# Deformable-convolution stage: the convolution moved ahead of the gathers, all row turns between the second and third spread, and the arguments of the offsets in two buffers

## The chip, the cores and the metric

The kernel is written by hand for one core of a Trainium2 chip, in fp32 throughout. The metric is device time in microseconds of one execution. The kernel before was timed three times: median 1808.21 us, 1806.97 to 1809.94.

A core has a matrix engine (TensorE, PE in the profile), whose weight loads are listed apart (PEld), and three engines for elementwise work: VectorE (DVE), ScalarE (ACT) and GpSimd (POOL). SyncE (SP) only issues DMAs here. Every engine has its own stream of instructions, and streams meet at semaphores alone. Small scalar instructions (register arithmetic, branches, semaphore waits that stand by themselves) are carried out by the engine's sequencer, which hands matmuls and weight loads on to the engine.

## What is computed

`x` is 8 x 32 x 128 x 128. Two residual layers follow each other, each on a normalized input:

```python
x = x + _L0_conv_ref(_gn(x), ...)   # spectral terms along H and W, and a 1x1 mix of channels
x = x + _L1_conv_ref(_gn(x), ...)   # deformable 3x3 convolution

# _L1_conv_ref, cut:
om = conv3x3(x, w_om) + b_om                    # 27 maps: 18 offsets, 9 masks
off, mask = om[:, :18], sigmoid(om[:, 18:])
ys, xs = off + tap + pixel                      # a sampling point for every tap and pixel
vals = bilinear(x, ys, xs) * mask               # all 32 channels
out = einsum('bckhw,ock->bohw', vals, weight) + bias
```

The change touches only the second layer.

## The kernel before

The eight images go in two groups of four, so that 4 images x 32 channels fill the 128 partitions. After the first layer (about the first 180 us) a pipeline of 130 steps runs, 65 for each group (64 pairs of image rows and one more to finish). A step works on several pairs at once, in different stages. In step N:

- `offsets(N+3)` (L1122): the 3x3 convolution for the 27 maps, into the PSUM bank `pM`. ACT adds the bias (L655), `turn_offsets` (L1132) turns the result so that pixels stand on partitions, ACT takes the sigmoid of the masks (L666), and DVE subtracts the grid from the offsets, into `U` (L889). That is called the *subtraction* below.
- For pair N+2, ACT makes the bilinear hats from `U`: absolute value in place (L645) and 1 minus it, cut at zero, into `HT` (L648). POOL multiplies them by the masks (L546) and makes the products of the y hats and x hats (`product`, L511).
- For pair N+1, DVE turns the products (`turn`, L838).
- For pair N, three `spread` stages (L1076) lay the turned coefficients out as matrices in the PSUM tile `pE`, and ACT and DVE copy each of them, half each, into `A` (`table`, L633 and L832). POOL cuts the input window into strips (`cut_tiles`, L523), PE turns them in four *turns* (`turn_rows`, L1110, into `pR` or `pVV`), and ACT copies these into `XT` (`turned`, L638). Then three `gather` groups (L1097, of 6, 5 and 5 tiles) multiply `XT` by `A`; ACT and DVE copy the result out (`samples`, L628 and L827).
- For pair N-1, `convolve` (L1156) applies the 3x3 weights into `pVV`, and DVE adds bias, input and the part begun before (`output`, L849 and L854). DVE's increment of `conv_read` frees `pVV`.

Nothing plans this at run time: each engine's order is written out by hand in its `step` function. On PE it was: spread 0, convolve (N-1), spread 1, offsets (N+3), spread 2, turns 2 and 3 of N, turn_offsets, gather groups 0 to 2, turns 0 and 1 of N+1. On PE the steps 2 to 126 are one hardware loop with one step as its body, and the first and last steps are written out (`steps`, L282 to L307); DVE and SP have two steps in a loop body, ACT and POOL four. At the end of a body the sequencer runs an addition, a compare-and-branch and a further register instruction at L304.

Which PSUM banks a stage uses is given by these two lines; a group in `pV` (the two banks of `pVV`) has to wait for `output`, and one in `pE` for the tables of the third spread:

```python
pG = [pV, [pE[:, 0:512], pE[:, 512:1024]], [pE[:, 1024:1536], pE[:, 1536:2048]]]
pT = [pR, pV[0], pV[0], pR]
```

## Time and profile before

| | |
|---|---|
| median of 3 runs | 1808.21 us |
| the profiled execution | 1805.23 us, of which the span is 1803.3 us |
| PE busy | 94% of the span |
| DVE / ACT / POOL busy | 74% / 65% / 49% |
| step of the loop, spread 0 to the next spread 0 | 1006.82 to 1018.59 us: 11.77 us |
| granted TensorE clock | full from about 275 us to 1763 us |

PE's busy share counts every moment at which some matmul is in flight, so it hides the time in which the array waits between two stages. What a stage costs is read here from the start of its first matmul to the start of the next stage's first matmul; these numbers add up to the step without gap or overlap. Instructions of the sequencer are not in the engine rows; the view of one source line lists them (as PEldq for PE).

### The profile page before, as it was taken

What the parts mean: (1) busy time and instruction counts of PE and PEld (TensorE: products, weight loads), DVE (VectorE), ACT (ScalarE), POOL (GpSimd) and SP (SyncE); (2) the same over time, 40 slices, a digit from 0 to 9 for tenths busy, and PEclk for the clock granted to TensorE, in tenths of its full rate; (3) what the DMA queues carried; (4) which work ended last, traced back from release to release, by engine and by line L of the source; (5) the groups of instructions that cost most, each with busy time, mean ns of one, the idle gap of its engine ahead of it and who ended that gap; (6) DMA issues with size and microseconds to landing.
All of it is one profiled execution on the core that took longest, in us unless ns stands there. A gap on an engine that the chain in (4) does not pass through costs nothing.

```text
span 1803.3 us, 159696 instructions
## 1 busy us (share of the span) xinstructions
PE 1703.3 (94%) x70913; PEld 1319.3 (73%) x70913; DVE 1329.7 (74%) x2056; ACT 1174.5 (65%) x1971; POOL 891.7 (49%) x1153
## 2 busy tenths in 40 slices
PE   8886479999999999999999999999999999999985
PEld 3521257888888888888888888888888888888874
DVE  7387457777777777777777777777777777777762
ACT  7148246667767667777667677667677677676652
POOL 0000245556555556555556555555555565555550
PEclk9799599999999999999999999999999999999997
DMA  9148632333333333333333233333333333333320
GB/s 385 26 186 364 228 120 74 98 97 87 88 93 97 97 96 87 88 95 97 97 95 89 81 94 97 97 93 87 89 96 97 97 89 88 93 96 97 97 57 13
DMA packets 161679, 195.95 MB, mean 109 GB/s; under 512 B 20288, under 2 KB 136672, under 8 KB 157536
## 3 DMA queue, kind: packets, MB, share of 16 engines
q1 hardware_dynamic: 161632, 195.34, 36.6%
q8 instruction: 28, 0.46, 0.1%
q14 instruction: 19, 0.16, 0.0%
HBM read 143.05 MB, written 52.22 MB: 108 GB/s over the span
## 4 chain that ended last, share of the span: by engine, by line
PE 90%; DMA 3%; DVE 2%; issue 2%; ACT 1%; POOL 0%; DVEq 0%; SPq 0%; POOLq 0%; ACTq 0%
PE pE L1076 18%; PE pVV L1156 16%; PE pE L1097 13%; PE pM L1122 10%; PE pVV L1097 8%; PE pR L1110 7%; PE pVV L1110 7%; PE pM L1132 4%; PE pE L991 3%; DMA xh_scratch<-stg 2%; PE pE L1048 1%; DMA win<-xh_scratch 1%; DVE big L799 1%; ACT stg L592 1%; PE pVV L1026 0%
## 5 line engine op out<-in xcount | busy, mean ns | idle before, releaser
L523 POOL COPY big<-win 128x480 f32<-128x480 f32 x520 | 290.6, 588 | 654.5 <-PE pVV L1110 438.3
L511 POOL TENSOR_TENSOR prod<-big 128x600 f32<-128x600 f32 (+1 forms) x489 | 498.5, 1040 | 29.6 <-POOL big L546 29.5
L633 ACT ACTIVATE big<-pE 128x768 f32<-128x768 f32 x390 | 334.8, 858 | 186.8 <-PE pE L1076 186.8
L832 DVE COPY big<-pE 128x768 f32<-128x768 f32 x390 | 372.9, 956 | 100.1 <-PE pE L1076 87.5
L838 DVE STREAM_TRANSPOSE big<-prod 128x768 f32<-128x768 f32 x390 | 377.4, 968 | 15.8 <-POOL prod L511 15.8
L1076 PE MATMUL pE<-big,sel_s 32*64 32x192 f32 x12480 | 358.8, 338 | 12.5 <-DVE big L832 10.3
L1076 PEld LDWEIGHTS pE<-big,sel_s 32*64 32x64 f32 x12480 | 220.2, 132 | 115.7 <-issue 64.0
L1156 PE MATMUL pVV<-big,wc 64*32 64x128 f32 x18720 | 295.7, 273 | 4.3 <-issue 3.3
L1156 PEld LDWEIGHTS pVV<-big,wc 64*32 64x32 f32 x18720 | 263.2, 106 | 46.5 <-issue 46.3
L1097 PE MATMUL pE<-big 60*32 60x72 f32 x20800 | 251.4, 232 | 17.1 <-issue 17.1
L1097 PEld LDWEIGHTS pE<-big 60*32 60x32 f32 x20800 | 230.2, 105 | 24.2 <-issue 18.9
L1122 PE MATMUL pM<-big,wom 96*32 96x256 f32 x3120 | 201.3, 391 | 19.7 <-DMA big<-xh_scratch 19.7
L827 DVE COPY big<-pE 128x360 f32<-128x360 f32 x260 | 138.5, 533 | 105.0 <-PE pE L1097 105.0
L628 ACT ACTIVATE big<-pE 128x360 f32<-128x360 f32 x260 | 122.4, 471 | 123.0 <-PE pE L1097 123.0
L638 ACT ACTIVATE big<-pR 128x512 f32<-128x512 f32 x260 | 156.3, 601 | 23.3 <-PE pR L1110 8.6
L1110 PE MATMUL pR<-ident,big 128*128 128x128 f32 x1040 | 165.0, 282 | 6.5 <-POOL big L523 4.6
L1122 PEld LDWEIGHTS pM<-big,wom 96*32 96x32 f32 x3120 | 89.0, 110 | 104.6 <-issue 58.4
L1110 PE MATMUL pVV<-ident,big 128*128 128x128 f32 x1040 | 165.1, 282 | 0.0
L827 DVE COPY big<-pVV 128x432 f32<-128x432 f32 x130 | 79.0, 608 | 112.9 <-PE pVV L1097 111.0
L1097 PE MATMUL pVV<-big 60*32 60x72 f32 x12480 | 156.5, 230 | 4.5 <-ACT big L638 2.0
L638 ACT ACTIVATE big<-pVV 128x512 f32<-128x512 f32 x260 | 153.2, 589 | 0.9 <-PE pVV L1110 0.8
L1097 PEld LDWEIGHTS pVV<-big 60*32 60x32 f32 x12480 | 137.5, 105 | 11.3 <-issue 5.4
(97 smaller groups left out, 1675.7 us busy)
## 6 DMA issues: line engine op xcount, KB each, us to landing
big<-xh_scratch SPq DMA_DIRECT2D x390, 136.0 KB
win<-xh_scratch SPq DMA_DIRECT2D x130, 408.0 KB, 3.7
xh_scratch<-stg SPq DMA_DIRECT2D x32, 544.0 KB, 3.4
big<-in_x SPq DMA_DIRECT2D x16, 1024.0 KB, 15.7
x_scratch<-big SPq DMA_DIRECT2D x16, 1024.0 KB, 4.4
x1r<-x_scratch SPq DMA_DIRECT2D x256, 64.0 KB, 3.0
out<-outs SPq DMA_DIRECT2D x256, 64.0 KB, 2.1
xh_scratch<-zero SPq DMA_DIRECT2D x4, 204.0 KB, 2.6
```

The lines of the kernel that those rows point to most:

```text
L511: made = nc.gpsimd.tensor_tensor(prod[:, kx, at:at + m, 0:SQ].rearrange("p m (a b) -> p m a b", a=NSH), hy.to_broadcast(shape), hx.to_broa ...
L523: last = nc.gpsimd.tensor_copy(strips[:, half * HTP:(half + 1) * HTP, h, 0:REG].rearrange("p t (r x) -> p t r x", r=WIN_R), tiles_of(q, h, ...
L633: nc.scalar.activation(*expanded(kx, 0), ACT.Copy).then_inc(e_read, 1)
L638: nc.scalar.activation(XT[:, k * 512:(k + 1) * 512], pT[k][:, 0:512], ACT.Copy).then_inc(xt_done, 1)
L827: nc.vector.tensor_copy(*evacuate(gi, 1)).then_inc(v_dve, 1)
L832: nc.vector.tensor_copy(*expanded(kx, 1)).then_inc(e_read, 1)
L838: nc.vector.transpose(PT[:, kx, :], prod[:, kx, :, :].rearrange("p m k -> p (m k)")) \
L1076: last = mm(o[:, i2::TILE_R], sel_s[part, i2 * KS + kx, :], src[:, i2::TILE_R, :, h * NTP:(h + 1) * NTP], start=True, stop=True)
L1097: last = mm(o[:, :, x:x + TILE_C, :], XT[part, t * P + b * C:t * P + (b + 1) * C], A[part, b * NTP + t, :], start=True, stop=True)
L1110: last = nc.tensor.transpose(pT[k][:, u * P:(u + 1) * P], strips[:, k * TPC + u, :, :].rearrange("p h x -> p (h x)"), ident[:, :])
L1122: last = mm(pM[b * C:(b + 1) * C, 0:PX], wom[:, kx, :], wino[0:KS * C, b, :, x0:x0 + W], start=(kx == 0), stop=(kx == KS - 1))
L1156: last = mm(pV[r][to:to + C, c:c + W], wc[part, PLACES[at][1] * KS + kx, o * C:(o + 1) * C], VS[part, m, kx, :], start=(at == same[0] and ...
```

## The change

Each of the five streams is put in another order, and four details follow from it:

- PE: spread 0, offsets (N+3), spread 1, turns 0, 1 and 2 of N, turn_offsets, turn 3, spread 2, convolve (N-1), gather groups 0, 1, 2. All four turns now belong to the pair of the step. Gather groups 0 and 1 go to `pE`, group 2 to `pV`; turn 2 goes to `pV[1]`.
- `U` has two buffers, and DVE makes the subtraction in the middle of its step, before the third table, not at its end. `output` goes from behind the first turn to behind the third.
- ACT makes the absolute value as before and the cut at zero (L648 before, L667 now) late in the step, behind the third table.
- POOL cuts the strips after the second and third product; SP loads the rows for the offsets one pair further ahead and later in its step.
- The first spread waits for the copies of all gather groups but the last; the last gather group waits for `conv_read`, and each gather group has its own wait on `xt_done`.

```diff
-        pG = [pV, [pE[:, 0:512], pE[:, 512:1024]], [pE[:, 1024:1536], pE[:, 1536:2048]]]
-        pT = [pR, pV[0], pV[0], pR]
+        pG = [[pE[:, 0:512], pE[:, 512:1024]], [pE[:, 1024:1536], pE[:, 1536:2048]], pV]
+        pT = [pR, pV[0], pV[1], pR]
...
# POOL, step
-                    cut_tiles(N + 1, 1 - s % 2, 0)
                     product(N + 1, (s + 1) % RING, 1)
                     product(N + 1, (s + 1) % RING, 2)
+                    cut_tiles(N + 1, 1 - s % 2, 0)
+                    cut_tiles(N + 1, 1 - s % 2, 1)
...
# DVE, step
-                if on[-1]:
-                    output(N - 1, 1 - s % 2, place)
                 if on[0]:
                     table(N, 1)
...
+                if on[3]:
+                    dve.wait_ge(msk_done, N + 4)
+                    wait(dve, lin_done, N + 2)
+                    wait(dve, reach_done, N + 2)
...
                 if on[1]:
                     turn(N + 1, 2)
+                if on[-1]:
+                    output(N - 1, 1 - s % 2, place)
...
# PE, spread
                 if kx == 0:
-                    wait(pe, v_act, n * NG)
-                    wait(pe, v_dve, n * NG)
+                    wait(pe, v_act, n * NG - 1)
+                    wait(pe, v_dve, n * NG - 1)
# PE, gather
                 if gi == 0:
+                    pe.wait_ge(e_read, (n * ROUNDS + ROUNDS) * 2)
+                if gi == NG - 1:
                     wait(pe, conv_read, n)
-                    pe.wait_ge(e_read, (n * ROUNDS + ROUNDS) * 2)
-                    pe.wait_ge(xt_done, n * TCH + 3)
-                    pe.nop(nofuse=True)
-                if gi == 1:
-                    pe.wait_ge(xt_done, n * TCH + TCH)
-                    pe.nop(nofuse=True)
+                pe.wait_ge(xt_done, n * TCH + 2 + gi)
+                pe.nop(nofuse=True)
...
# PE, step
                 if on[0]:
                     spread(N, 0)
+                if on[3]:
+                    offsets(N + 3)
+                if on[0]:
+                    spread(N, 1)
+                    for k in range(TCH - 1):
+                        turn_rows(N, k)
+                if on[3]:
+                    turn_offsets(N + 3)
+                if on[0]:
+                    turn_rows(N, TCH - 1)
+                    spread(N, 2)
                 if on[-1]:
                     convolve(N - 1)
                 if on[0]:
-                    spread(N, 1)
-                if on[3]:
-                    offsets(N + 3)
-                if on[0]:
-                    spread(N, 2)
-                    turn_rows(N, 2)
-                    turn_rows(N, 3)
-                if on[3]:
-                    turn_offsets(N + 3)
-                if on[0]:
                     for gi in range(NG):
                         gather(N, gi)
-                if on[1]:
-                    turn_rows(N + 1, 0)
-                    turn_rows(N + 1, 1)
```

The end of the loop body on PE, before: from the last matmul of `turn_offsets` through the gather groups (L1097) and the two turns (L1110) to the branch.

```order
L1132 MATMUL pM<-perm_s,om_s 128x9x4
L1085 REGISTER_ALU [waits conv_read]
L1086 REGISTER_ALU [waits e_read]
L1097 MATMUL pVV<-big 32x3x4x6 [waits xt_done]
L1097 MATMUL pVV<-big 32x3x4x6 x47
L1089 REGISTER_ALU
L1097 MATMUL pE<-big 32x3x4x6 [waits xt_done]
L1097 MATMUL pE<-big 32x3x4x6 x79
L289 ISA
L1104 ISA [waits xt_done]
L1110 MATMUL pR<-ident,big 128x128 [waits strips_done]
L1110 MATMUL pR<-ident,big 128x128 x3
```

The same place in the changed kernel, from the convolution (L1158) through the gather groups (L1096) to the branch.

```order
L1158 MATMUL pVV<-big,wc 32x128 x71
L1085 REGISTER_ALU
L1088 REGISTER_ALU [waits e_read]
L1096 MATMUL pE<-big 32x3x4x6 [waits xt_done]
L1096 MATMUL pE<-big 32x3x4x6 x47
L1088 REGISTER_ALU
L1096 MATMUL pE<-big 32x3x4x6 [waits xt_done]
L1096 MATMUL pE<-big 32x3x4x6 x39
L1088 REGISTER_ALU [waits conv_read]
L1096 MATMUL pVV<-big 32x3x4x6 [waits xt_done]
L1096 MATMUL pVV<-big 32x3x4x6 x39
L304 REGISTER_ALU
```

The gathers have one more place at which a register instruction and a wait cut their row of matmuls, and the loop's branch has moved from behind eight turns of 128 x 128 to right behind the last gather matmul.

The middle of the loop body on PE, before: spread 2 (L1076), turns 2 and 3 (L1110), `turn_offsets` (L1132).

```order
L1076 MATMUL pE<-big,sel_s 64x3x64 x15
L289 ISA
L1104 ISA [waits xt_done]
L1110 MATMUL pVV<-ident,big 128x128 [waits conv_read,strips_done]
L1110 MATMUL pVV<-ident,big 128x128 x3
L1110 MATMUL pR<-ident,big 128x128 [waits strips_done,xt_done]
L1110 MATMUL pR<-ident,big 128x128 x3
L1128 REGISTER_ALU
L1132 MATMUL pM<-perm_s,om_s 128x9x12 [waits om_act]
```

And now: behind spread 1 (L1077) come three turns (L1112), `turn_offsets` (L1134) and the fourth turn.

```order
L1112 MATMUL pR<-ident,big 128x128 x3
L1112 MATMUL pVV<-ident,big 128x128 [waits v_dve,v_act]
L1112 MATMUL pVV<-ident,big 128x128 x3
L1110 REGISTER_ALU
L1112 MATMUL pVV<-ident,big 128x128 [waits strips_done]
L1112 MATMUL pVV<-ident,big 128x128 x3
L1130 REGISTER_ALU
L1134 MATMUL pM<-perm_s,om_s 128x9x12 [waits om_act]
L1134 MATMUL pM<-perm_s,om_s 128x9x8
L1134 MATMUL pM<-perm_s,om_s 128x9x4
L1108 REGISTER_ALU
L1112 MATMUL pR<-ident,big 128x128 [waits xt_done]
```

The stages with 128 x 128 weights stood in two blocks and stand in one.

On DVE, the second half of a step before: third table (L832), third turn (L838), the copies of the gathers (L827), the subtraction (L889).

```order
L832 COPY big<-pE 128x2x64x6 [waits e_done]
L836 REGISTER_ALU
L838 STREAM_TRANSPOSE big<-prod 128x768 [waits e_done,prod_done]
L827 COPY big<-pVV 128x18x24 [waits v_done]
L827 COPY big<-pE 128x18x20 [waits v_done] x2
L883 REGISTER_ALU
L889 TENSOR_TENSOR big<-pM,cols_s 128x720 [waits reach_done,lin_done,msk_done]
```

And now: the subtraction (L880), third table (L831), third turn (L837), `output` (L848, L853), the copies (L826).

```order
L880 TENSOR_TENSOR big<-pM,cols_s 128x720 [waits reach_done,lin_done,msk_done]
L831 COPY big<-pE 128x2x64x6 [waits e_done]
L835 REGISTER_ALU
L837 STREAM_TRANSPOSE big<-prod 128x768 [waits e_done,prod_done]
L848 SCALAR_TENSOR_TENSOR outs<-pVV,bias_s,begun 128x256 [waits out_st1,conv_done]
L853 TENSOR_TENSOR begun<-pVV,x1r 128x256 [waits x1_ld1]
L826 COPY big<-pE 128x18x24 [waits v_done]
L826 COPY big<-pE 128x18x20 [waits v_done]
L826 COPY big<-pVV 128x18x20 [waits v_done]
```

Subtraction and `output` now both stand in the row of DVE work between the third spread and the gathers.

## Rows read from the trace of the kernel before

**Rows 1.** The page, groups: line, engine, count | busy us, mean ns of one | idle before.

```profile
L1097 PE MATMUL pE<-big 60*32 60x72 f32 x20800 | 251.4, 232 | 17.1 <-issue 17.1
```

**Rows 2.** Waits, 275 to 1740 us: engine, line, waited for, us in total, times, longest.

```profile
PEld pE L1076 <- DVE big L832: 51.1, 124, 0.4
```

**Rows 3.** Timeline of PE, one step: start us, length, line, output and input, count.

```profile
1006.82 0.91 PE L1076 MATMUL pE<-big,sel_s 32*64 32x192 f32 x32
1007.72 2.24 PE L1156 MATMUL pVV<-big,wc 64*32 64x128 f32 x144
1009.89 0.91 PE L1076 MATMUL pE<-big,sel_s 32*64 32x192 f32 x32
1010.73 1.50 PE L1122 MATMUL pM<-big,wom 96*32 96x256 f32 x24
1012.16 0.91 PE L1076 MATMUL pE<-big,sel_s 32*64 32x192 f32 x32
1013.00 0.66 PE L1110 MATMUL pVV<-ident,big 128*128 128x128 f32 x4
1013.49 0.60 PE L1110 MATMUL pR<-ident,big 128*128 128x128 f32 x4
1013.92 0.76 PE L1132 MATMUL pM<-perm_s,om_s 128*128 128x108 f32 x6
```

**Rows 4.** Timeline of PE, rest of that step and next spread; first row: last three of turn_offsets.

```profile
1014.21 0.47 PE L1132 MATMUL pM<-perm_s,om_s 128*128 128x72 f32 x3
1014.65 1.21 PE L1097 MATMUL pVV<-big 60*32 60x72 f32 x96
1015.75 1.88 PE L1097 MATMUL pE<-big 60*32 60x72 f32 x160
1017.56 0.66 PE L1110 MATMUL pR<-ident,big 128*128 128x128 f32 x4
1018.05 0.60 PE L1110 MATMUL pVV<-ident,big 128*128 128x128 f32 x4
1018.59 0.73 PE L1076 MATMUL pE<-big,sel_s 32*64 32x192 f32 x22
```

**Rows 5.** PEld: weight loads of gather groups 1 and 2, same step.

```profile
1015.72 1.73 PEld L1097 LDWEIGHTS pE<-big 60*32 60x32 f32 x160
```

**Rows 6.** PE's sequencer, 1014.4 to 1019.6 us: ns shortest/median/longest, first and last start.

```profile
L304 PEldq COMPARE_BRANCH  x1: 207/207/207, 1017.7 to 1017.7; - x1
L304 PEldq FUSED_REGOPS  x1: 59/59/59, 1018.0 to 1018.0; - x1
...
L289 PEldq FUSED_REGOPS  x2: 37/37/37, 1017.3 to 1018.9; - x2
L289 PEldq EVENT_SEMAPHORE  x2: 51/51/51, 1017.5 to 1018.2; - x2
```

**Rows 7.** PE's branch over all steps of the loop.

```profile
L304 PEldq COMPARE_BRANCH  x125: 76/208/223, 275.9 to 1736.5; - x125
```

**Rows 8.** Timeline of ACT and DVE in the step before.

```profile
1001.43 0.96 DVE L832 COPY big<-pE 128x768 f32<-128x768 f32 x1
...
1002.30 0.97 DVE L838 STREAM_TRANSPOSE big<-prod 128x768 f32<-128x768 f32 x1
...
1005.10 0.53 DVE L827 COPY big<-pE 128x360 f32<-128x360 f32 x1 [0.25 <-PE pE L1097]
...
1006.36 0.90 DVE L889 TENSOR_TENSOR big<-pM,cols_s 128x720 f32<-128x720 f32 x1
...
1006.99 0.59 ACT L638 ACTIVATE big<-pVV 128x512 f32<-128x512 f32 x1
```

**Rows 9.** Timeline at the first steps: masks, third subtraction, first table.

```profile
206.34 0.23 ACT L666 ACTIVATE msk<-pM 128x72 f32<-128x72 f32 x1 [1.59 <-PE pM L1132]
...
214.58 0.86 DVE L889 TENSOR_TENSOR big<-pM,cols_s 128x720 f32<-128x720 f32 x1
...
219.93 0.95 DVE L832 COPY big<-pE 128x768 f32<-128x768 f32 x1
```

More of the change, by code:

```diff
@@ L106, in build @@
         PT = areas[3].rearrange("p (s n) -> p s n", s=KS)
-        U = areas[4]
+        U = [areas[4][:, q * UW:(q + 1) * UW] for q in range(2)]
         HT = areas[5].rearrange("p (f s n) -> p f s n", f=2 * KS, s=RING)
@@ L424, in step @@
                 q = s % 2
-                if isinstance(N, int) and N + 3 == NSET:
-                    sp.wait_ge(x1_st[1], 16 * LOADS)
-                    for b in range(2):
-                        sp.wait_ge(xh_st[b], 16 * N_XH)
-                if on[3]:
-                    load_rows(N + 3, place)
+                if on[1]:
+                    load_window(N + 1, 1 - q, place)
                 if isinstance(N, int):
@@ L442, in step @@
                             .then_inc(x1_ld[q], 16)
+                if isinstance(N, int) and N + 4 == NSET:
+                    sp.wait_ge(x1_st[1], 16 * LOADS)
+                    for b in range(2):
+                        sp.wait_ge(xh_st[b], 16 * N_XH)
+                if not isinstance(N, int) or N + 4 < SETS:
+                    load_rows(N + 4, place)
                 g, local = place(N - 1)
@@ L668, in step @@
                 if on[0]:
+                    turned(N, TCH - 1)
+                    table(N, 2)
+                if on[2]:
+                    act.wait_ge(abs_done, N + 3)
+                    wait(act, prod_done, N * KS)
+                    nc.scalar.activation(HT[:, :, (s + 2) % RING, :],
+                                         U[s % 2].rearrange("p (f n) -> p f n", f=2 * KS), ACT.Relu,
+                                         bias=cols_s[:, 1:2], scale=-1.0).then_inc(lin_done, 1)
+                if on[0]:
                     for gi in range(NG):
                         samples(N, gi)
-                if on[1]:
-                    turned(N + 1, 0)
-                    turned(N + 1, 1)
             steps(act, step, RING)
@@ L1101, in turn_rows @@
             def turn_rows(n, k):
-                wait(pe, xt_done, n * TCH + k - k % 2)
-                pe.wait_ge(strips_done, n * 2 + (k // 2 + 1))
+                if k == 0:
+                    wait(pe, xt_done, n * TCH)
                 if k == 1:
-                    wait(pe, v_act, (n - 1) * NG + 1)
-                if k == 2:
-                    wait(pe, conv_read, n)
+                    wait(pe, v_act, n * NG)
+                    wait(pe, v_dve, n * NG)
+                if k == 3:
+                    pe.wait_ge(xt_done, n * TCH + 1)
+                if k % 2 == 0:
+                    pe.wait_ge(strips_done, n * 2 + (k // 2 + 1))
                 for u in range(TPC):
@@ L1139, in convolve @@
                 pe.wait_ge(v_dve, n * NG + NG)
-                wait(pe, xt_done, min((n + 1) * TCH + 2, SETS * TCH) if isinstance(n, int) else n * TCH + (TCH + 2))
+                wait(pe, xt_done, min((n + 1) * TCH + 3, SETS * TCH) if isinstance(n, int) else n * TCH + (TCH + 3))
                 pe.nop(nofuse=True)
@@ L1163, in step @@
                     spread(N, 0)
+                if on[3]:
+                    offsets(N + 3)
+                if on[0]:
+                    spread(N, 1)
+                    for k in range(TCH - 1):
+                        turn_rows(N, k)
+                if on[3]:
+                    turn_offsets(N + 3)
+                if on[0]:
+                    turn_rows(N, TCH - 1)
+                    spread(N, 2)
                 if on[-1]:
```

40 lines of the change are left out of this document (13 added, 27 removed).

## The prediction

> **What bounds the kernel now.** I read the page's costliest groups first, all of them PE's and the copies behind it, then the list of waits inside the loop, then one step of PE's timeline row by row, and last the sequencer's instructions around the branch. In the list of waits the entries of PE and PEld are small: the largest with an engine's name is the spread behind DVE's table, 51.1 us over 124 steps or 0.41 each [rows 2]. In the timeline the reader is to see that PE goes from stage to stage: the step is 11.77 us long, and its stages, each from its first matmul to the first matmul of the next, are [rows 3, 4]:
>
> - spread 0 to convolve 0.90, convolve to spread 1 2.17, spread 1 to offsets 0.84, offsets to spread 2 1.43, spread 2 to turns 0.84;
> - first turn of a block 0.49, second 0.43, turn_offsets 0.73, gather group 0 1.10, groups 1 and 2 1.81;
> - turns 0 and 1: 0.49 and 0.54.
>
> They add up to 11.77. Even the 0.41 us of [rows 2] is no real wait: spread 2 starts 1.43 us behind offsets, and the offsets' own matmuls run 1.50 us [rows 3]. So the step is a sum of PE's stages, and the change moves time only where a border between two stages costs something else than before, or where a wait appears. The branch comes 125 times, from 275.9 to 1736.5 us [rows 7], or every 11.78 us (124 intervals).
>
> **Borders with a change of weight shape.** The first matmul of the second turn comes 0.49 us after that of the first turn when the block begins behind a spread or a gather, and the next stage of 128 x 128 follows the second turn after 0.43; the last turn before a spread takes 0.54 [rows 3, 4]. A turn in the middle of a block thus costs 0.43 to 0.44, one at its front 0.05 more, one at its end 0.10 more. Now all four turns and turn_offsets are one block: 0.49, 0.44, 0.43, turn_offsets, 0.54. For turn_offsets I need its cost with a turn behind it. Its fourth product starts 0.29 us behind its first (1014.21 against 1013.92), which makes 0.58 for six [rows 3, 4]; the upper bound is the 0.73 it takes now, the lower one 0.44, a turn of four instructions. I take 0.58, which reads its own products. The block is then 0.49 + 0.44 + 0.43 + 0.58 + 0.54 = 2.48, against 0.49 + 0.43 + 0.73 + 0.49 + 0.54 = 2.68: **0.20 us saved**. The other stages in front of the gathers keep their neighbours' shapes: spread to offsets 0.84, offsets to spread 1.43, spread to turns 0.84. Spread to convolve stays 0.90, or 0.87 if the last 0.03 against the other spreads was the wait for the copy of a turn (ACT L638 ends at 1007.58, convolve starts at 1007.72 [rows 3, 8]), which now is done long before. I take 0.87.
>
> Convolve to gather is a border that the trace doesn't show. Convolve has 64-row weights, the gathers 60-row ones, both of 32 columns. The bounds are 2.17, what convolve takes before a spread, and 2.00, if nothing at all came between. But three sequencer instructions stand at this border now (two register instructions, one wait), and such an instruction takes the sequencer about 0.1 us: the ones behind the gathers start at 1017.3, 1017.4 and 1017.5 [rows 6], the middle one, at L1104, between the two of L289. I take 2.14, the end near the row.
>
> The Trainium skill, "TensorEngine Tiling (Array Packing)", section "Key Properties", says that a change of tiling mode drains the engine and a change of tile alone does not. The rows agree in kind (0.05 and 0.10 us more at the ends of a block). By that rule this border would be of the second sort, and the change would pay two mode changes fewer in a step; my sum gives it only 0.03, since the sequencer is late there.
>
> **Borders where the sequencer is late.** This is the part that costs. In the gathers PE takes a weight load and a matmul each 0.011 us (160 loads in 1.73 us [rows 5]). The last loads start at about 1017.34, and the first sequencer instruction behind them starts at 1017.3 [rows 5, 6]: the sequencer has almost no lead there, so that whatever it does next, PE waits for.
>
> - One more border inside the gathers. Group 0 has 96 matmuls; at 0.0103 us each (160 in 1.88, less the 0.23 of the last one's own length [rows 1, 4]) they take 0.99, but group 1 starts 1.10 behind [rows 4]. So the register instruction and the wait between groups 0 and 1 cost 0.11. Groups 1 and 2 had none between them; they now have. **+0.10**, between 0 and 0.2.
> - The branch. Before, it began at 1017.7, under eight turns' matmuls that run until 1018.59, and hid. Now it stands behind the last gather. Its chain is an addition (about 0.1 us, as above), the branch (207 ns), 0.3 behind its start at 1017.7 a register instruction at 1018.0, a wait, and the first weight load [rows 6]. With the two of 0.1 for wait and load that is 0.1 + 0.3 + 0.2 = 0.6, of which I take 0.57, since the starts are rounded to 0.1. Before, the first turn stood 0.25 us behind the sequencer's first instruction (1017.56 against 1017.3). So the spread starts **0.32 us later** behind the gathers than the turn did. The bounds: 0 if the sequencer gets ahead, 0.45 if the wait's 1018.2 was its natural time.
>
> The Trainium skill, "Advanced Engine Details and Errata", section "Control Flow Timing", gives a compare-and-branch about 108 ns; the trace shows 208 ns as the median of 125 [rows 7]. With 0.11 in place of 0.21 the exposed part would be 0.22 and the step 0.10 shorter; the measurement decides.
>
> The sum of the new step: 0.84 + 1.43 + 0.84 + 2.48 + 0.87 + 2.14 + 1.10 + 1.81 + 0.10 + 0.32 = 11.93 (spread 0, offsets, spread 1, block, spread 2, convolve, gathers, border, branch), against 11.77: **+0.16 us**. Before has small waits beyond this step's (11.78 on the mean), after I expect fewer; I count +0.15. Over 125 steps of the loop: +18.8 us.
>
> **What hides the rest.** Moved waits, counted from spread 0 = 0. Offsets end at about 2.3, spread 1 at 3.1; ACT does its second table (at most DVE's 0.96) and three copies of turns (0.59 each [rows 8]) by about 5.8, the sigmoid by 6.0. DVE's subtraction (0.90) then runs to 6.9, the third table (0.96) to 7.9, the third turn (0.97) to 8.8 [rows 8]. The first gather starts at 8.6 and needs the table at 7.9: 0.7 to spare, 0.5 after the semaphores. `output` follows convolve's end (8.7); its two operations on 256 columns are each shorter than the 0.53 of 360 columns [rows 8], so `conv_read` comes by 9.9; group 2 starts at 10.7. The first spread of the next step needs DVE's copy of group 1, which ends 0.6 behind group 1, and PE comes 1.3 behind it. `wino` is loaded from 2.4 on for offsets that start at 12.8; the window is ordered behind `output` and is needed by POOL 5 us later. On SP the out DMAs now stand behind a wait on offsets of the same step, which ends before `output` does. None of these takes time; the cover is thinnest at the third table.
>
> **First steps.** DVE's subtraction of the third pair, at 214.58, waited behind a turn whose product POOL made only after the window had landed, though its masks were ready at 206.57; the first table followed 5.35 later at 219.93 [rows 9]. With products ahead of the strips it can start at 206.6, one turn (0.97) moves behind it, so the table comes at about 213: I count -6, between -9 and 0.
>
> Together +18.8 - 6 = +12.8 on a profiled execution of 1805.23 us, which is 2.98 below the median of the runs. The same difference on the median gives 1821; rounded down for the chance of small savings, 1820.
>
> **The rivals.** (a) *The sequencer is not late behind the last gather group*, because that group waits a little and the queue fills. Then the 0.32 goes and the block's 0.20 stays: -0.17 a step, -21 - 6 = -27, 1781, faster. For it: in spreads and turns the sequencer does run ahead (the branch at 1017.7 stands 0.9 us before the spread it serves [rows 4, 6]). Against it: 1017.3 in the gathers. It decides as soon as less than 0.15 us of the branch is exposed. The Trainium skill, "TensorE: Matmul & The Clock Gate", section "Architectural detail", gives TensorE a queue of 64 instructions, which by itself would hide the branch behind the last 32 pairs of the gather. Chance 0.20. (b) *Half of it*: 0.20 exposed, or border and branch together 0.1 less: +0.05 a step and -6, 1808, no change. Chance 0.13. (c) *A new wait*: DVE's row of subtraction, table, turn and `output` comes late, and the gathers wait for the table or group 2 for `conv_read`. It needs 0.5 us of slip, and would then cost some 0.3 more a step: 1858. Chance 0.06. The forecast has 0.61, with 1812 to 1830 as its own range.
>
> About 0.2% (3.6 us) is what a measurement of this kernel can tell from no change. Faster takes (a) and a little of (b): 0.23; the same 0.13; slower 0.64. The range of 8 in 10 reaches from the lower part of the mixed cases, 1798, to 1832.
>
> **What would show it.** Right: a step of 11.9 us; in PE's timeline 0.45 to 0.5 us between the last gather matmul's start and the spread, with the branch inside it; group 2's first matmul 0.1 late; block 2.5 us. Wrong: no gap before the spread, or a wait on DVE's L831 or L853 before a gather, or convolve to gather well under 2.1.

## The result and the profile after

| | before | after |
|---|---|---|
| median of 4 runs each | 1807.59 us (1806.3 to 1809.94) | 1841.72 us (1840.0 to 1842.4) |
| ratio after to before | | 1.0186, 95% interval 1.0168 to 1.0204 |
| profiled execution | 1805.23 us, span 1803.3 | 1842.1 us, span 1839.7 |
| forecast | | 1820 us, range 1798 to 1832 |

The change makes the kernel slower, as forecast, but by 34 us where 13 were forecast; the time lies outside the range. The page of the changed kernel, the span, the busy shares and the chain that ended last:

```profile
span 1839.7 us, 159867 instructions
PE 1700.6 (92%) x70913; PEld 1329.5 (72%) x70913; DVE 1353.8 (74%) x2056; ACT 1144.2 (62%) x1971; POOL 896.9 (49%) x1153
PE 89%; issue 5%; DMA 3%; DVE 2%; ACT 1%; DVEq 0%; SPq 0%; ACTq 0%
```

The other engines have not become the bound. The granted clock of the loop is 1.00 before and after. The list of waits says the same in more detail; these are its two longest entries of PEld between 275 and 1740 us, as line, what ended the idle time, sum in us, times, longest:

```profile
PEld pE L1077 <- issue: 82.8, 241, 0.6
PEld pE L1077 <- DVE big L831: 49.9, 121, 0.4
```

The wait behind DVE's table is the one of [rows 2] again, 0.41 us a step as before. The other is "issue" in front of the spreads, that is PE's own sequencer: 82.8 us where the kernel before has 45.4, and what is new of it stands in front of spread 0. The remaining entries of PEld, in front of the other stages, are of 34 to 39 us before and after. Now one step of PE's timeline, the answer to [rows 3, 4] (start, duration, operation, tiles, shapes, count, idle time before it):

```profile
1003.56 0.91 PE L1077 MATMUL pE<-big,sel_s 32*64 32x192 f32 x32 [0.37 <-issue]
1004.40 1.50 PE L1124 MATMUL pM<-big,wom 96*32 96x256 f32 x24
1005.84 0.91 PE L1077 MATMUL pE<-big,sel_s 32*64 32x192 f32 x32
1006.67 0.66 PE L1112 MATMUL pR<-ident,big 128*128 128x128 f32 x4
1007.16 1.04 PE L1112 MATMUL pVV<-ident,big 128*128 128x128 f32 x8
1008.04 0.76 PE L1134 MATMUL pM<-perm_s,om_s 128*128 128x108 f32 x6
1008.63 0.63 PE L1112 MATMUL pR<-ident,big 128*128 128x128 f32 x4
1009.19 0.91 PE L1077 MATMUL pE<-big,sel_s 32*64 32x192 f32 x32
1010.03 2.25 PE L1158 MATMUL pVV<-big,wc 64*32 64x128 f32 x144
1012.16 2.19 PE L1096 MATMUL pE<-big 60*32 60x72 f32 x176
1014.24 1.07 PE L1096 MATMUL pVV<-big 60*32 60x72 f32 x80
1015.71 0.91 PE L1077 MATMUL pE<-big,sel_s 32*64 32x192 f32 x32 [0.41 <-issue]
```

From first matmul to first matmul: spread 0 0.84, offsets 1.44, spread 1 0.83, three turns 1.37, turn_offsets 0.59, turn 3 0.56, spread 2 0.84, convolve 2.13, gather groups 0 and 1 2.08, group 2 up to the next spread 1.47. That is 12.15 us. The last one is the conspicuous one. The sequencer's instructions in it, and PE's branch over the whole run (duration min/median/max, first and last start):

```profile
L304 PEldq ALU_OP  x1: 32/32/32, 1015.0 to 1015.0; - x1
L304 PEldq COMPARE_BRANCH  x1: 208/208/208, 1015.1 to 1015.1; - x1
L304 PEldq FUSED_REGOPS  x1: 59/59/59, 1015.3 to 1015.3; - x1
L289 PEldq ALU_OP  x1: 36/36/36, 1015.5 to 1015.5; - x1
L289 PEldq EVENT_SEMAPHORE  x1: 51/51/51, 1015.6 to 1015.6; - x1
```

```profile
L304 PEldq COMPARE_BRANCH  x125: 76/208/228, 261.5 to 1769.5; - x125
```

The branch comes every 12.16 us (124 intervals) against 11.78 before [rows 7]. Against before, the loop's 124 intervals take 47.5 us more (1508.1 against 1460.6), the part ahead of the first branch 14.4 less (261.5 against 275.9), and the part behind the last branch 3.3 more (70.2 against 66.9). Together 36.4 us, the difference of the two spans.

The loop's +0.38 per step, divided among the borders between stages, as means over the steps from a stage's first weight load to the next stage's:

| border | before | after | difference |
|---|---|---|---|
| block of 128 x 128 stages | 2.643 | 2.522 | -0.12 |
| convolve to the next stage (spread, now gather) | 2.198 | 2.109 | -0.09 |
| spread to convolve | 0.871 | 0.836 | -0.04 |
| spread to offsets (the spread now stands behind a gather) | 0.836 | 0.869 | +0.03 |
| gathers, first load to last load | 2.754 | 2.928 | +0.17 |
| last gather load to the next stage | 0.211 | 0.627 | +0.42 |

### The profile page after: what moved, and what is told of

It reads as the page before. It is cut to its first block, busy times and chain, and to the rows that moved or that the text cites. A ratio compares the mean times of both kernels' runs of the same rounds, so it can differ in the third digit from the quotient of the medians.

```text
span 1839.7 us, 159867 instructions
## 1 busy us (share of the span) xinstructions
PE 1700.6 (92%) x70913; PEld 1329.5 (72%) x70913; DVE 1353.8 (74%) x2056; ACT 1144.2 (62%) x1971; POOL 896.9 (49%) x1153
## 4 chain that ended last, share of the span: by engine, by line
PE 89%; issue 5%; DMA 3%; DVE 2%; ACT 1%; DVEq 0%; SPq 0%; ACTq 0%
PE pE L1077 18%; PE pVV L1158 16%; PE pE L1096 15%; PE pM L1124 10%; PE pR L1112 8%; PE pVV L1096 7%; PE pVV L1112 6%; PE pM L1134 4%; PE pE L992 3%; DMA xh_scratch<-stg 2%; PE pE L1049 1%; DVE big L798 1%; ACT stg L592 1%; PE pVV L1027 0%; DMA big<-xh_scratch 0%
## 5 line engine op out<-in xcount | busy, mean ns | idle before, releaser
L512 POOL TENSOR_TENSOR prod<-big 128x600 f32<-128x600 f32 (+1 forms) x489 | 493.1, 1041 | 29.6 <-POOL big L548 29.5
L831 DVE COPY big<-pE 128x768 f32<-128x768 f32 x390 | 373.1, 957 | 168.4 <-PE pE L1077 168.4
L1077 PE MATMUL pE<-big,sel_s 32*64 32x192 f32 x12480 | 358.5, 337 | 53.1 <-issue 46.8
L837 DVE STREAM_TRANSPOSE big<-prod 128x768 f32<-128x768 f32 x390 | 377.7, 969 | 0.0
L1077 PEld LDWEIGHTS pE<-big,sel_s 32*64 32x64 f32 x12480 | 224.4, 132 | 149.0 <-issue 96.6
L628 ACT ACTIVATE big<-pE 128x432 f32<-128x432 f32 (+1 forms) x260 | 130.3, 501 | 285.3 <-PE pE L1096 285.3
L1096 PE MATMUL pE<-big 60*32 60x72 f32 x22880 | 286.8, 230 | 14.6 <-issue 13.4
L1158 PE MATMUL pVV<-big,wc 64*32 64x128 f32 x18720 | 296.2, 272 | 3.3 <-issue 2.5
L1158 PEld LDWEIGHTS pVV<-big,wc 64*32 64x32 f32 x18720 | 259.8, 106 | 40.7 <-issue 40.7
L1096 PEld LDWEIGHTS pE<-big 60*32 60x32 f32 x22880 | 261.7, 105 | 37.2 <-issue 16.5
L826 DVE COPY big<-pE 128x432 f32<-128x432 f32 (+1 forms) x260 | 148.3, 570 | 95.7 <-PE pE L1096 95.6
L548 POOL TENSOR_TENSOR big<-big,msk 128x360 f32<-128x360 f32 x130 | 107.4, 826 | 211.0 <-ACT big L667 211.0
L1112 PE MATMUL pR<-ident,big 128*128 128x128 f32 x1040 | 170.1, 287 | 0.0
L1096 PE MATMUL pVV<-big 60*32 60x72 f32 x10400 | 144.3, 231 | 8.6 <-issue 8.6
L1112 PEld LDWEIGHTS pR<-ident,big 128*128 128x128 f32 x1040 | 121.7, 153 | 37.2 <-issue 36.9
L638 ACT ACTIVATE big<-pVV 128x512 f32<-128x512 f32 x260 | 142.6, 610 | 1.3 <-PE pVV L1112 1.3
L880 DVE TENSOR_TENSOR big<-pM,cols_s 128x720 f32<-128x720 f32 x130 | 118.0, 908 | 28.0 <-ACT msk L659 20.6
```

What stands on the lines that cost most here:

```text
L512: made = nc.gpsimd.tensor_tensor(prod[:, kx, at:at + m, 0:SQ].rearrange("p m (a b) -> p m a b", a=NSH), hy.to_broadcast(shape), hx.to_broa ...
L638: nc.scalar.activation(XT[:, k * 512:(k + 1) * 512], pT[k][:, 0:512], ACT.Copy).then_inc(xt_done, 1)
L826: nc.vector.tensor_copy(*evacuate(gi, 1)).then_inc(v_dve, 1)
L831: nc.vector.tensor_copy(*expanded(kx, 1)).then_inc(e_read, 1)
L837: nc.vector.transpose(PT[:, kx, :], prod[:, kx, :, :].rearrange("p m k -> p (m k)")) \
L1077: last = mm(o[:, i2::TILE_R], sel_s[part, i2 * KS + kx, :], src[:, i2::TILE_R, :, h * NTP:(h + 1) * NTP], start=True, stop=True)
```

## The experiments

Each kernel ran in three rounds or more against the kernel before, whose medians in these comparisons were 1806.1 to 1807.0 us; the ratios are to that. The theory: the branch stands exposed behind the last gather and costs 0.4 us a step, and the gathers' new border and something inside them the other 0.17. The rivals: the order of the stages (a wait on DVE or ACT, the shape of the block) makes the loss, or the sequencer's costs are there but can't be got back.

### e1: the branch moved under the turns

PE's loop body is cut in another place, the order of its instructions is the same:

```diff
-            steps(pe, step, 1)
+            # head: spread 0 to turn 3; tail: spread 2, convolve, gathers
+            with pe.Fori(0, SETS - 5) as j:
+                tail(j + 1, {k: True for k in range(-1, 4)})
+                head(j + 2, {k: True for k in range(-1, 4)})
```

> The changed kernel with its order on every engine untouched; only PE's loop body is cut at another place, so that the branch stands behind the fourth turn (as it did before the change) and not behind the last gather matmul. 125 iterations as before. Theory A (PE's sequencer is late behind the gathers and its branch chain of about 0.65 us is exposed): from the last gather weight load to the spread 0.21 to 0.31 us in place of 0.63, a step of 11.8 us in place of 12.16, time near 1798 us (1790 to 1806). Rival B (the spread waits there for the copies of the gathers by DVE and ACT, or gathers into another bank are slow): nothing changes, 1842 us. Rival C (the branch costs the same wherever the engine has less than 0.65 us of work queued): the gap moves behind the turns, time above 1830 us.

Measured: 1797.14 us, ratio 0.9948 [0.9931, 0.9964]; step 11.78. Its timeline around the gathers and around the new place of the branch, between turn 3 and spread 2:

```profile
1007.01 2.16 PE L1096 MATMUL pE<-big 60*32 60x72 f32 x176
1009.05 1.07 PE L1096 MATMUL pVV<-big 60*32 60x72 f32 x80
1010.11 0.91 PE L1077 MATMUL pE<-big,sel_s 32*64 32x192 f32 x32
...
1015.18 0.64 PE L1112 MATMUL pR<-ident,big 128*128 128x128 f32 x4
1015.74 0.91 PE L1077 MATMUL pE<-big,sel_s 32*64 32x192 f32 x32
```

Group 2 to spread 0 takes 1.06 instead of 1.47, and the gap marked "issue" is gone. Turn 3 to spread 2 takes 0.56, as it did without a branch. The order of PE's work is the same, so the 44.6 us between the two medians go with the place of the branch: the last gather load stands 0.247 us ahead of the spread on the mean, against 0.627, which is 0.38 a step. The loop's 124 intervals take 1460.6 us here, exactly what they take in the kernel before. The 9 us by which e1 is faster than that kernel lie in the steps that are written out around the loop.

### e3: the kernel before, with its branch behind the gathers

```diff
# PE, step
                 if on[0]:
+                    turn_rows(N, 0)
+                    turn_rows(N, 1)
...
-                if on[1]:
-                    turn_rows(N + 1, 0)
-                    turn_rows(N + 1, 1)
```

> The kernel before the change with its order untouched, but PE's loop body cut behind the last gather group instead of behind the two turns that follow it: only the place of the branch is that of the changed kernel. Theory A (exposed branch): the first turn starts 0.6 us behind the last gather weight load in place of 0.21, a step of 12.15 to 12.2 us, time near 1856 us (1845 to 1862). Rival B (the change of order, not the branch, costs the time): 1808 us.

Measured: 1849.13 us, ratio 1.0233 [1.0216, 1.025], 43 us above before. Its timeline behind the last gather group, and its branch:

```profile
1002.93 1.88 PE L1097 MATMUL pE<-big 60*32 60x72 f32 x160
1005.05 0.65 PE L1110 MATMUL pR<-ident,big 128*128 128x128 f32 x4 [0.25 <-issue]
```

```profile
L304 PEldq COMPARE_BRANCH  x125: 76/208/223, 277.2 to 1778.6; - x125
```

Gathers to turn takes 2.12 against 1.81 [rows 4]. The step is 12.11 us by the branch, 0.33 more than before, with the order of PE's work unchanged. Here the place of the branch alone, in an order that is otherwise the old one, makes the loss. In front of a turn it costs 0.315 us (0.526 against 0.211 from the last gather load), which is just what the prediction worked out (0.32) from the same rows of a turn; in front of spread 0 it costs 0.38.

### e2 and e4: one border less inside the gathers

The wait for `conv_read` goes ahead of group 1, all of `xt_done` is waited for ahead of group 0, and group 2 has no sequencer instruction; e2 is the changed kernel with this edit, e4 is e1 with it.

```diff
                 if gi == 0:
                     pe.wait_ge(e_read, (n * ROUNDS + ROUNDS) * 2)
-                if gi == NG - 1:
+                    pe.wait_ge(xt_done, n * TCH + TCH)
+                    pe.nop(nofuse=True)
+                if gi == 1:
                     wait(pe, conv_read, n)
-                pe.wait_ge(xt_done, n * TCH + 2 + gi)
-                pe.nop(nofuse=True)
+                    pe.nop(nofuse=True)
```

> The changed kernel with the waits of the gather groups put together: group 0 waits for the tables and all four turned pieces, group 1 for the freeing of the convolution's bank, group 2 for nothing, so that one register instruction and one wait between groups 1 and 2 are gone. Theory A (a sequencer instruction between gather groups is exposed, since the sequencer has no lead there): the stretch from group 1's first weight load to group 2's goes from 0.99 back to 0.82 us, time 0.15 x 125 = 19 us less, 1823 us (1817 to 1829). Rival B (the border costs because group 2 waits for DVE's output operations): the wait now stands ahead of group 1 and costs there at least as much, 1842 to 1870 us.

> The changed kernel with both of the others: branch behind the fourth turn, and no instruction between gather groups 1 and 2. If both costs are the sequencer's and independent they add: a step of 11.65 us and a time near 1779 us (1771 to 1788), below the kernel before. If they are one wait seen at two places, the time is that of the better of the two alone. If another engine (DVE's row of subtraction, table, turn and output) becomes the bound once PE is faster, 1790 to 1800 us with waits on DVE in the list.

Measured: e2 1844.04 us, ratio 1.02 [1.0183, 1.0217], no gain on the changed kernel; e4 1801.07 us, ratio 0.9968 [0.9956, 0.9979], no gain on e1. Theory A of e2 and the sum that e4 was to give were missed; e2's time lies in the range of its rival B, the wait that moves ahead of group 1. The weight loads of e2 (PEld) show what became of the border:

```profile
1003.15 2.04 PEld L1097 LDWEIGHTS pE<-big 60*32 60x32 f32 x175
...
1005.10 1.02 PEld L1097 LDWEIGHTS pVV<-big 60*32 60x32 f32 x79
```

Between groups 1 and 2 the loads now follow each other without a gap, where the border with a register instruction and a wait takes 0.142 us instead of 0.012 from load to load. So the border's 0.13 is real and gone. But from first load to last the gathers still take 2.932 us, against 2.928. Two things give the 0.13 back. Ahead of group 1 there is now 0.07 us more on the mean: in 56 of 124 steps the interval there is 0.28 us long, and group 1's first load then starts 0.11 us behind the end of DVE's `output` each time, so it waited for `conv_read`. That is rival B's wait, at about half the saving. The rest are pauses within the groups. A pause here is an interval between two gather loads, inside a group, that is at least 0.04 us longer than the usual one at its place; most are about 0.08 us long. Between the loop's first and last branch the changed kernel has 0.79 of them a step, e2 1.69; before has 0.63, e1 0.98, e4 1.71. They were in neither theory, and e5 and e10 were made for them. (The expectations of e5 and e10 count pauses a little wider: 1.0 a step in e1.)

### e5 and e10: SyncE's issues out of the gathers

In the changed kernel DVE's `output` ends within the gathers, and what SyncE waits for it then issues at once. SyncE's issues in the changed kernel, around the gathers that start at 1012.16 (the next spread starts at 1015.71):

```profile
1012.89 1.25 SPq L448 DMA_DIRECT2D out<-outs  x2
1014.24 0.55 SPq L404 DMA_DIRECT2D win<-xh_scratch  x1
1014.88 1.30 SPq L435 DMA_DIRECT2D x1r<-x_scratch  x2
```

Of the x1r loads between 275 and 1740 us only 8 of 238 are issued in the first 3 us behind the first gather load, that is while the gathers run. In the kernel before it is the other way round: its two output stores are issued at 1010.57, under spread 1 and offsets, and its x1r loads in the gathers or just ahead of them (these start at 1014.65 [rows 4]):

```profile
1014.17 1.31 SPq L441 DMA_DIRECT2D x1r<-x_scratch  x2
```

e5 is e1 with the stores held back until spread 0 of the next step is done; what follows them on SyncE moves with them:

```diff
# SP, step
                     sp.wait_ge(out_ready, N - 1 - g)
                     sp.nop(nofuse=True)
+                    if not isinstance(N, int) or N + 1 < SETS:
+                        sp.wait_ge(e_done, N * ROUNDS + (ROUNDS + 1))
+                        sp.nop(nofuse=True)
```

> e1 (branch under the turns), and SyncE additionally waits for the first spread of the next step before it issues the two stores of the output, so that these, and the window and input loads queued behind them, are issued during spread and offsets and no longer during the gathers. Same DMAs, same order. Theory A (the pauses of about 0.08 us among the gathers' weight loads come from DMA work that SyncE starts in that stretch, as their closeness to its issues in e2 suggests): the gathers go from 2.956 us (first to last weight load, mean) to 2.88 or less, time 1797 - 9 = 1788 us. Rival B (the pauses have another source, such as the ends of ACT's and DVE's copies): nothing changes, 1797 us. Rival C (the loads now come late for the strips or for output): slower than 1797.

e10 is e1 with only the loads of window and x1r held back, until spread 0 is done; the stores stay in the gathers:

```diff
# SP, step
                 if on[1]:
+                    if not isinstance(N, int) or N > 0:
+                        sp.wait_ge(e_done, N * ROUNDS + 1)
+                        sp.nop(nofuse=True)
                     load_window(N + 1, 1 - q, place)
```

> e1 (branch under the turns), with SyncE's wait for the first spread put behind the two output stores and ahead of the window and input loads: the stores are issued as in e1, during the gathers, and only the loads are kept out of them. In e5 both were kept out and the pauses went (0.03 a step against 1.0). If the loads make the pauses: as e5, 1789 us, gathers 2.90 us. If the stores make them: as e1, 1797 us, gathers 2.95 us. If each makes its share, in between, with the pauses at the first half of the gathers left.

Measured: e5 1789.38 us, ratio 0.9916 [0.9894, 0.9939]; in its loop no pause is left, the gathers take 2.870 us (e1 2.926) and the step 11.73. e10 1797.75 us, ratio 0.9945 [0.9928, 0.9962]; 0.95 pauses a step, just like e1. In e10 the stores fall in the gathers again. SyncE's issues and PE's gathers of e5:

```profile
998.31 1.30 SPq L451 DMA_DIRECT2D out<-outs  x2
```

```profile
997.26 0.91 PE L1080 MATMUL pE<-big,sel_s 32*64 32x192 f32 x32
998.10 1.50 PE L1127 MATMUL pM<-big,wom 96*32 96x256 f32 x24
...
1005.87 2.16 PE L1099 MATMUL pE<-big 60*32 60x72 f32 x176
...
1009.00 0.91 PE L1080 MATMUL pE<-big,sel_s 32*64 32x192 f32 x32
```

The same of e10, where the stores come 0.7 us into the gathers:

```profile
1021.70 1.29 SPq L451 DMA_DIRECT2D out<-outs  x2
```

```profile
1020.96 2.17 PE L1099 MATMUL pE<-big 60*32 60x72 f32 x176
```

So in the changed order the pauses come with the output stores, and these cost 8 us over the run. That loads are harmless is not shown. e10 is no test of it, since in e1 they are issued almost wholly behind the gathers, and the kernel before speaks against it: all 78 of its pauses in the loop stand 0.93 to 1.06 us behind the start of an x1r load's issue on SyncE, just as all 98 of the changed kernel stand 0.94 to 1.06 us behind that of an output store. Loads of the window, issued just ahead of the old gathers, have no pause behind them (0 of 115). That x1r loads make the old pauses is argued from this spacing; no run moved them. The change thus brought the stores into the gathers and took the x1r loads out, and the pauses went only from 0.63 to 0.79 a step. In e2, with one border less, they stand behind most stores. What in such a transfer disturbs PE (its issue, its access to SBUF, its packets) wasn't tried.

### e6: branch, border and stores together

e6 is e4 with the stores held back as in e5.

> e4 (branch under the turns and no instruction between gather groups 1 and 2) with the same delay of SyncE as e5. Theory A (what the missing border saves in e2 and e4 is given back by pauses tied to DMA issues): gathers of 2.80 us, time 1797 - 0.15 x 125 = 1778 us (1774 to 1784). Rival B (pauses of another source): 1801 us as e4. The wait for the convolution's bank ahead of group 1 (0.07 us in e2) stays under both.

Measured: **1782.77 us** (1778.63 to 1783.32), ratio 0.987 [0.9846, 0.9894], step 11.65. It is 1.3% faster than the kernel before. The list of its waits between 300 and 1720 us has this of the gathers:

```profile
PEld pE L1100 <- issue: 13.2, 58, 2.2
```

From first load to last the gathers take 2.754 us in the median step of the loop and 2.796 on the mean, the 2.80 of theory A. Only 0.02 pauses a step remain; what lies above the median is the wait for `conv_read` in front of group 1, again an interval of 0.28 us in 56 of 124 steps. With the stores out of the way the missing border does pay: e6 is 6.6 us under e5, where e4 was not under e1. The 58 idle times of the list are 0.23 us long on the mean; the longest, 2.2 us, falls in a step written out behind the loop, whose last branch comes at 1698.2.

### e7: the fourth turn apart from the block

This measures what a change of weight shape costs. e7 is e1 with turn 3 behind spread 2, and ACT's copy of it behind the third table:

```diff
# PE
-                    turn_rows(N, TCH - 1)
                     spread(N, 2)
+                    turn_rows(N, TCH - 1)
# ACT
-                    turned(N, TCH - 1)
                     table(N, 2)
+                    turned(N, TCH - 1)
```

> e1, with the fourth turn moved from behind the turning of the offsets to behind the third spread (on ScalarE its copy follows the third table), so that the stages of 128 x 128 weights stand in two blocks as before the change; the branch then stands behind the turning of the offsets. Theory A (a block has an edge cost of 0.10 to 0.16 us, the gain of the change in the steady step): +0.15 us a step, 1797 + 19 = 1816 us (1809 to 1822). Rival B (edges cost nothing, the saving of the block was something else): 1797 us.

Measured: 1810.53 us, ratio 1.0029 [1.0017, 1.004], 13.4 above e1; step 11.897, +0.117. The timeline of e7:

```profile
1009.53 0.76 PE L1134 MATMUL pM<-perm_s,om_s 128*128 128x108 f32 x6
1010.22 0.91 PE L1077 MATMUL pE<-big,sel_s 32*64 32x192 f32 x32
1011.05 0.66 PE L1112 MATMUL pR<-ident,big 128*128 128x128 f32 x4
1011.64 2.25 PE L1158 MATMUL pVV<-big,wc 64*32 64x128 f32 x144
```

turn_offsets in front of a spread takes 0.69, in front of a turn 0.59; a turn that stands alone 0.59, at the end of a block 0.56. So two more changes of shape, with ACT's copy moved to match, cost 0.12 to 0.13, not the 0.15 of the forecast's edges (0.05 at the front and 0.10 at the end), and the 13.4 us lie inside the range that was given, near its lower end.

### e8: the first steps as before

The order of the first steps, which are written out ahead of the loop, is made that of before for SyncE's window and POOL's strips; the branch stays where the changed kernel has it.

```diff
# SP, step
-                if on[1]:
+                early = isinstance(N, int) and N < 2
+                if on[1] and not early:
                     load_window(N + 1, 1 - q, place)
...
+                if on[1] and early:
+                    load_window(N + 1, 1 - q, place)
# POOL, step
+                early = isinstance(N, int) and N < 0
+                if on[1] and early:
+                    cut_tiles(N + 1, 1 - s % 2, 0)
                     product(N + 1, (s + 1) % RING, 1)
                     product(N + 1, (s + 1) % RING, 2)
-                    cut_tiles(N + 1, 1 - s % 2, 0)
-                    cut_tiles(N + 1, 1 - s % 2, 1)
+                    if not early:
+                        cut_tiles(N + 1, 1 - s % 2, 0)
+                        cut_tiles(N + 1, 1 - s % 2, 1)
...
+                if on[1] and early:
+                    cut_tiles(N + 1, 1 - s % 2, 1)
```

> The changed kernel with GpSimd's order of strips and products put back in the steps ahead of step 0, and SyncE's order of window load and stores put back in the steps ahead of step 2; the loop is untouched. Theory A (the changed kernel's first steps are shorter because products and turn no longer wait for the first window): the first table comes 5 to 7 us later, the loop's first branch 5 to 15 us later than its 261.4 us, time 1842 + 5 to 15 = 1847 to 1857 us. Rival B (the gain at the start comes from PE's own order): within 2 us of 1842.

Measured: 1846.93 us (1844.73 to 1849.36), ratio 1.0228 [1.0205, 1.025], 5.2 above the changed kernel's median and just under theory A's range; in the trace:

```profile
L304 PEldq COMPARE_BRANCH  x125: 76/208/232, 269.7 to 1777.8; - x125
```

The first branch comes 8.2 us later than in the changed kernel (261.5), the loop's 124 intervals take 1508.1 us as there. The first table comes at 219.71, 6.4 later than the 213.33 of the changed kernel. So 8 of the 14.4 us at the start are the order of strips, products and window.

## Why the prediction was off

**The direction, the bound and the place were right.** The profile was read as a sum of PE's stages plus what the sequencer can't hide. This held: no wait on DVE or ACT appeared, the border inside the gathers and the branch behind them are where the time went, and the idle time before spread 0, with the branch inside it, is the sign that the prediction gave, only larger: 0.63 us from the last gather load to the spread's first. The prediction is at odds with itself here: its sum works with 0.57, its list of signs has 0.45 to 0.5. Rival (a), a sequencer that isn't late, would have had no such gap; rival (c), a new wait on DVE, is excluded by the list of waits. e1 and e3 show the branch as the cause from both sides.

**The step that failed is the sum "borders where the sequencer is late": +0.10 for the border and +0.32 for the branch, which measured +0.17 and +0.42.** In its parts:

- *Branch exposure, 0.32 forecast, 0.42 measured.* The chain was counted as an addition, the branch, one register instruction, a wait and the load, 0.57 together. The rows after show a second register instruction of L289, at 1015.5, between the first and the wait: the chain is 0.65 from the addition to the load, and the load stands 0.63 behind the last gather load instead of 0.57. The 0.32 had been taken from rows in which a turn follows, and for a turn it is right to 0.01, but not by the chain that was counted. In e3 two register instructions stand ahead of the turn's first load (at 1005.04), and the wait comes behind it:

```profile
L1104 PEldq FUSED_REGOPS  x1: 37/37/37, 1005.0 to 1005.0; - x1
L1104 PEldq EVENT_SEMAPHORE  x1: 51/51/51, 1005.1 to 1005.1; - x1
```

So what spread 0 has more than a turn is the wait ahead of its first load, 0.10 us (0.627 against 0.526 from the last gather load). Of this, 0.04 is there without a branch too (0.247 ahead of a spread, 0.211 ahead of a turn); the other 0.06 makes the branch cost 0.38 in front of spread 0 (e1) and 0.315 in front of a turn (e3). The upper bound of 0.45 did hold the 0.42. That the wait makes the difference is read from these rows; it wasn't tried alone.

- *Extra border in the gathers, 0.10 forecast, 0.17 measured.* The border by itself is 0.13 (0.142 us against 0.012 from load to load), close to its 0.10 and inside its bounds. Nearly all of the other 0.04 lies in group 1: 0.847 us from its first load to its last, where the kernel before takes 0.805 and e5, without the stores, 0.816. So some 0.03 of it are pauses that go with the output stores. The prediction looked up where SyncE's stores move and asked only whether someone waits for them; it found no wait, which is true, and had no term for what they do to a stage in which PE has no slack.
- *The block's 0.20 saved, 0.12 to 0.16 measured.* By first matmuls it is 2.52 against 2.68, by weight loads 2.522 against 2.643. turn_offsets (0.59 for 0.58), the front and the end of the block (0.49, 0.56) are near the forecast's single values; the small excesses (0.01 at turn_offsets, 0.02 at turn 3) add up. e7 gives the same size from the other side, 0.12 for two edges of a block.
- *Convolve to gather, 2.14 forecast, 2.11 to 2.13 measured.* Right, and *spread to convolve* likewise (0.84 for 0.87).
- *The first spread* takes 0.03 more from its first weight load to that of the next stage; this had no term. It isn't the branch: e1 has the same 0.869, so it comes with the gather in front of the spread.

**The step in sum**: 12.16 against the forecast's 11.93, of which the branch is 0.10, the gathers 0.07 and the block 0.04; rounding and small terms are the rest. Over 125 steps the excess is 29 us.

**First steps, -6 forecast, -14.4 measured.** The mechanism is the one named: POOL makes the products from 199.19 on, ahead of the strips at 203.50, and DVE's subtraction and first table move up. The rows that answer to [rows 9], after:

```profile
206.60 0.88 DVE L880 TENSOR_TENSOR big<-pM,cols_s 128x720 f32<-128x720 f32 x1
213.33 0.95 DVE L831 COPY big<-pE 128x768 f32<-128x768 f32 x1
```

The first table comes at 213.33 instead of 219.93, or 6.6 us earlier, the size that was forecast. The other 7.8 us arise between this table and the first branch: 48.1 us against 55.9, and 50.0 in e8, so that the order of strips and products explains about 2 of them. In the kernel before these steps have idle times of PE marked "issue" of 0.75 to 2.79 us, outside any loop; the changed kernel's second step already gained 9.1 (its spread 0 at 226.39 against 235.53). The granted clock differs as well. Between the table and the branch it is at the lower of its two levels (0.5, 1.2 GHz) for 13.6 us before, for 4.9 in the changed kernel and for 9.5 in e8. Before, it falls at 243.8 and at 260.8, close to idle times of PE of 2.20 us (up to 242.02) and 2.79 us (up to 260.88), and the spread of 244.04 then takes 1.58 us instead of 0.91. What of this is cause and what follows from the other order stays open, and with it about 6 us.

**The end** takes 3.3 us more, for which the forecast had 0; the last steps hold exposed gather borders as well, and the granted clock is at its lower level for 41 of the last 70 us, against 30 of 67 before. It was not taken apart.

**Some luck.** The loop alone is 29 us above the forecast. The time is only 22 us above it, since the first steps gave back 8 us more than forecast, for reasons that the prediction did not have, and the end took 3 of them.

**Why the hidden steps cost nothing**, as forecast. DVE's row after: subtraction, third table, third turn and `output` all come ahead of the stages that need them.

```profile
1009.31 0.91 DVE L880 TENSOR_TENSOR big<-pM,cols_s 128x720 f32<-128x720 f32 x1
1010.21 0.96 DVE L831 COPY big<-pE 128x768 f32<-128x768 f32 x1
1011.08 0.97 DVE L837 STREAM_TRANSPOSE big<-prod 128x768 f32<-128x768 f32 x1
1012.33 0.48 DVE L848 SCALAR_TENSOR_TENSOR outs<-pVV,bias_s,begun 128x256 f32<-128x256 f32 x1 [0.28 <-PE pVV L1158]
1012.73 0.41 DVE L853 TENSOR_TENSOR begun<-pVV,x1r 128x256 f32<-128x256 f32 x1
```

The table that the gathers need ends at 1011.17, the gathers start at 1012.16. `conv_read` comes at 1013.14, group 2 starts at 1014.24. The prediction had given 0.7 us of cover for the table and 0.8 for `conv_read`; it was 1.0 and 1.1.

**The range** ended at 1832, though the prediction's own bounds for the two sequencer terms, 0.45 and 0.20, stand 0.23 us above the values taken. Over 125 steps that is 29 us, or 1849; a range that took both in would have held the time.

## What to carry to other kernels

Put the loop's branch, and every register instruction and wait that can be moved, behind instructions that take the array long compared to their issue, never behind a row of short matmuls that run at issue speed: there the sequencer had no lead, and the branch's chain of 0.65 us cost 0.32 to 0.38 us a pass. When a chain of the sequencer is priced from rows, count the instructions that stand in front of the first load of the *stage that will follow*, the wait among them, not those of the stage that followed before. And when transfers move, ask not only who waits for them, but under which work they fall: here a stage at issue speed felt them though nothing waited.

## What the runs showed of the hardware

- Behind the gathers, where the sequencer has no lead, the branch's chain takes 0.65 us from its addition to the next weight load (medians of the starts: 0.10 to the branch, 0.27 to the register instruction behind it, 0.12 to the second, 0.10 to the wait, 0.08 to the load), of which the branch's own 208 ns are a third. Under turns of 128 x 128 the same branch cost nothing that could be measured (0.56 us from turn 3 to spread, with or without it).
- A register instruction and a wait between two gather groups cost 0.13 us (0.142 from load to load instead of 0.012).
- Output stores issued by SyncE during the gathers cost PE about one pause of 0.08 us a step, with no semaphore between them (0.98 a step in e1, none in e5, which only issues them later). In the kernel before, where x1r loads are issued there instead, 0.63 pauses a step stand at the same distance behind these, about 1.0 us behind the start of the issue.
- More of these pauses came when a border was taken out (0.79 to 1.69 a step in e2), and only with the stores moved away did that border pay (6.6 us in e6).
